# GpSimd's scatter of edge sums waits for 24 of 98 merging steps, in place of the first

## What is computed

```
h = relu(layernorm(x)); x = x + L0(h, edges)          # two rounds of messages, summed per node, then a GRU cell
h = relu(layernorm(x)); x = x + L1(h, edges, weight)  # weighted sum over the edges of a node
h = relu(layernorm(x)); x = x + L2(h, src, dst)       # attention: softmax over the edges of a node
h = relu(layernorm(x)); x = x + L3(h, edges)          # mean over the edges of a node, two dense products
...
agg[n] = sum of msg[e] over the edges e with dst[e] == n
```

## Time and profile before

| | |
|---|---|
| time, three runs | 3922.49, 3908.88, 3908.34 us; median 3908.88 |
| span of the profiled execution | 3922.1 us |
| the run nearest to that span | 3922.49 us, 0.4 above it |
| GpSimd's scatter, first to last start | 71.0 to 1168.1 us |
| merging steps, first to last `summed` | 70.6 to 1113.9 us |
| table loads begin (L428) | 1187.05 us |

### The profile page before, as it was taken

One profiled execution on the slowest core, in us unless ns is written; L12 is line 12 of the kernel. 1 busy time (PEld: TensorE's weight loads), 2 busy tenths in 40 slices (PEclk: granted clock), 3 DMA queues, 4 the chain that ended last, 5 costly groups with the idle time before them and its releaser, 6 DMA issues.

```text
span 3922.1 us, 37110 instructions
## 1 busy us (share of the span) xinstructions
PE 2203.3 (56%) x11497; PEld 1368.2 (35%) x11497; DVE 1745.8 (45%) x2706; ACT 981.7 (25%) x1791; POOL 1607.2 (41%) x1664
## 2 busy tenths in 40 slices
PE   3111111111113666678989677777777777777389
PEld 2000000000001132454544455555555555555245
DVE  6121112111126223343423367666666666766742
ACT  0000000000001322200110145555555555555311
POOL 2766666666670000002000455555555555555300
PEclk7555555555555778878999788888888888888689
DMA  9999200000003978763358577777887777777443
GB/s 389 368 333 366 90 1 2 1 1 2 1 6 137 403 297 325 266 190 96 109 188 259 163 209 215 215 218 212 221 225 211 211 218 213 217 213 217 130 134 113
DMA packets 509104, 724.18 MB, mean 185 GB/s; under 512 B 70756, under 2 KB 366621, under 8 KB 509008
## 3 DMA queue, kind: packets, MB, share of 16 engines
q1 hardware_dynamic: 437444, 608.72, 47.2%
q0 software_dynamic: 65680, 109.05, 10.9%
q10 hardware_dynamic: 5884, 5.21, 0.4%
HBM read 402.27 MB, written 320.51 MB: 184 GB/s over the span
## 4 chain that ended last, share of the span: by engine, by line
PE 36%; another core or an unknown queue 28%; DVE 12%; issue 9%; DMA 8%; ACT 7%; SPq 0%; ACTq 0%; POOL 0%; DVEq 0%; POOLq 0%
PE PS L677 8%; DMA G<-adj_d 7%; PE PS L981 5%; PE PS L951 4%; PE PS L960 4%; PE PS L976 3%; PE PS L1006 2%; DVE V L1648 2%; PE PS L811 2%; PE PS L975 1%; DVE V L1649 1%; ACT OSF L1266 1%; ACT M L1259 1%; ACT D L1277 1%
## 5 line engine op out<-in xcount | busy, mean ns | idle before, releaser
L595 POOL DMA_INDIRECT G<-tab_sv,src_e x784 | 768.3, 980 | 648.7 <-PE PS L677 395.5
L605 POOL DMA_INDIRECT adj_d<-D,place x782 | 752.9, 963 | 410.3 <-issue 240.7
L733 PE MATMUL PS<-G,V 128*128 128x4 bf16 x391 | 41.8, 171 | 885.3 <-issue 488.5
L981 PE MATMUL PS<-M,ident 128*128 128x512 f32 x392 | 272.7, 785 | 334.3 <-ACT M L1259 247.4
L733 PEld LDWEIGHTS PS<-G,V 128*128 128x128 bf16 x391 | 33.6, 104 | 973.0 <-issue 529.2
L1656 DVE TENSOR_REDUCE D<-PS 128x8 f32<-128x24 f32 x98 | 17.5, 178 | 714.7 <-remote 710.8
L1955 DVE TENSOR_TENSOR_SCAN RB<-mring,RB,PS 128x512 f32<-128x512 bf16 x196 | 250.3, 1277 | 139.3 <-PE PS L981 132.6
L1935 DVE TENSOR_TENSOR_SCAN HTx<-PS,HTx,D 128x512 f32<-128x512 f32 x196 | 250.9, 1280 | 90.7 <-remote 49.2
L976 PE MATMUL PS<-VT 128*128 128x128 f32 x1568 | 287.1, 285 | 0.0
L595 POOL DMA_INDIRECT wlast<-wsum_d,last_i x25 | 23.9, 957 | 627.7 <-DVE last_i L1867 620.4
L1266 ACT ACTIVATE OSF<-PS 128x512 f32<-128x512 f32 x392 | 212.3, 593 | 269.9 <-PE PS L677 160.6
(11 more groups left out here) (402 smaller groups left out, 4694.3 us busy)
## 6 DMA issues: line engine op xcount, KB each, us to landing
frac_d<-OSF SPq DMA_DIRECT2D x196, 512.0 KB
adj_d<-RB SPq DMA_DIRECT2D x7, 12800.0 KB, 44.0
G<-adj_d SPq DMA_DIRECT2D x161, 512.0 KB, 6.1
run_d<-RB SPq DMA_DIRECT2D x4, 12992.0 KB
VT<-run_d SPq DMA_DIRECT2D x196, 256.0 KB
wts_d<-X SPq DMA_DIRECT2D x149, 256.0 KB, 6.3
mring<-cut_d SPq DMA_DIRECT2D x196, 128.0 KB
HTx<-seg_d SPq DMA_DIRECT2D x196, 128.0 KB
```

The costliest lines, as they stand in the source:

```text
L595: pool.indirect_dma_start(dest, None, table, bass.IndirectOffsetOnAxis(ap=idx, axis=0)).then_inc(done, 16)
L605: pool.indirect_dma_start(adj_d, bass.IndirectOffsetOnAxis(ap=place[:, 2 * w + k:2 * w + k + 1], axis=0), pay[:, w, k, :], None).then_inc( ...
L981: nc.tensor.matmul(PS[:, q, :], ident[:, :], Ee[:, q, :], start=False, stop=True, skip_group_check=True).then_inc(leaky, 1)
```

## The change

GpSimd's wait for `summed` before a window of a new step asks for at least 24. The first DMA of the scatter so waits for 24 merging steps (96 of 391 windows) in place of one, and all waits up to the 24th step are met from then on. From the 24th step on each wait asks for what it asked before. No instruction is added, removed or moved on any engine.

```diff
@@ -62,6 +62,7 @@
 NU = 2 * NSG
 NP = -(-NW // 4)
+AHEAD = 24
 PC = 512
@@ -616,7 +617,7 @@
                     for w in windows(u):
                         if w % 4 == 0 or w == windows(u)[0]:
-                            pool.wait_ge(summed, w // 4 + 1)
+                            pool.wait_ge(summed, max(w // 4 + 1, AHEAD))
                         issue(0, u, w)
```

## The result

| | before | changed |
|---|---|---|
| median of five runs | 3908.88 us | 3954.48 us |
| lowest to highest | 3896.95 to 3922.52 | 3936.16 to 3960.43 |
| span of the profiled run | 3922.1 us | 3934.4 us |
| scatter, first to last start | 71.0 to 1168.1 | 115.5 to 1213.3 |

The change makes the kernel slower: ratio 1.0102, 95% interval 1.0066 to 1.0138, 45.6 us between the medians. The two profiled runs are 12.3 us apart only: that of the changed kernel was the fastest of its five, that of before lay 13.6 above its median. The scatter's end says more than the spans do: it moved by 45.3 us.

A forecast was written before the change was run, and what follows sets the result against it. The prediction took the scatter to be bound by GpSimd's own issuing, with merging a tenth of it. A start 43.5 us later and 41 us of saved pauses gave +2 us, a forecast of 3911 us, range 3885 to 3953.

The forecast's parts named there:

- The likeliest case, no change: Whole kernel: late start and saved pauses nearly cancel, +2 us, time 3911 us; chance of "same" 0.61.
- slow rival: Scatter: the start costs its 43.5 us and nothing comes back, 3952 us; chance 0.21.
- What bounds the kernel: Scatter of edge sums: bound by GpSimd's own issuing, a tenth by merging; its end moves later loads and layers one for one.
- The start: GpSimd's first scatter DMA: waits for 24 merging steps at 1.89 us, begins at 114.5 in place of 71.0, +43.5 us.
- The pauses saved: Scatter up to the 286th DMA: GpSimd doesn't pause until the margin is used up, -41 us.
- The meeting point: Scatter: GpSimd catches up with merging at step 38, the 286th DMA, at 475 us.
- about one instruction for each of its DMAs: Merging beside the unbroken scatter: TensorE completes that many after a reserve of four or five quick steps; 36 us a step taken.
- From the meeting on both kernels stand alike: no margin, a pause every some 50 DMAs, to the end: Scatter after the 286th DMA: nothing differs but the phase, one pause of up to 8 us more or less.
- a mild form of the slow rival: Scatter after the meeting: GpSimd's later pauses grow by more than 18 us; counted within the slow rival's 0.21.
- The slow rival's own mechanism: Merging: the profiler's recording holds TensorE's completions; in timed runs merging stays ahead at 1.89 us a step, without pauses.
- Merging keeps up: Scatter: with the margin GpSimd never pauses, +43.5 - 110 = -67 us, 3842 us; chance 0.17.

The follow-up runs named there:

- few24: The changed kernel with the third small matmul of each window left out, 20 TensorE instructions a merging step in place of 28; 3966.21 us, ratio to before 1.0115.
- a48b: The kernel before with GpSimd's first wait asking for 48 merging steps, on the third chip, which holds TensorE; 4029.41 us, ratio to before 1.0196.
- before2: The kernel before, unchanged, profiled again on the first chip, which doesn't hold TensorE; 2885.29 us, ratio to itself 0.9996.
- few1: The kernel before with the third small matmul of each window left out, 20 TensorE instructions a merging step; 3949.15 us, ratio 1.0000.
- before3: The kernel before, unchanged, executed once for a third profile on the third chip, which holds TensorE; 3945.0 us.

## Why the prediction was right or wrong

The forecast was 3911 with a range of 3885 to 3953, the measured median 3954.5: 1.5 above the range's end by these five runs, within it by the ratio (3908.9 x 1.0102 = 3948.8). The likeliest case, no change, was wrong; the slow side, given 0.21, came. That the range reached so far up is not to the account's credit: it was stretched for a slow rival whose mechanism isn't what the runs showed (5).

1. *What bounds the kernel*: right on a chip that holds TensorE. The scatter's end moved by 45.3 us and the time by about as much (34 to 46 us in two sessions). One for one it holds only within the 20 us by which the chain behind the scatter varies (18, 37 and 17 us in three profiles).
2. *The start*: forecast +43.5, measured +44.5; 1.89 us a step held for 24 steps in a row.
3. *The pauses saved*: forecast 41 us up to the 286th DMA, measured 28.6 up to the 288th. The meeting point was right (286 and 288), but by luck: the steps took 39.2 us where I took 36, which alone puts the meeting at about the 277th DMA, and GpSimd's own slowing put it back. The term was mis-sized because I let GpSimd run at 1.263 us a DMA: 375.4/288 is 1.303, since in a long stretch it too is slowed. few24's 20 DMAs in 28.0 us and a48b's 336 in 470.4 show that slowing by itself. The prediction's "about one instruction for each of its DMAs" is wrong too: the price is 1.40 us an instruction, with 31 DMAs in a step of 28 instructions as with 28.
4. *"From the meeting on both kernels stand alike: no margin, a pause every some 50 DMAs, to the end"*: this is the step that failed. The runs showed a debt there: pauses of 14.6 and 14.7 us in the changed kernel, three in few24, one of 21 and one of 7 in a48b, after which GpSimd was as late as its start had been. In place of "alike", the changed kernel's first 302 DMAs ended with the whole 45.3 us of the late start, and the scatter's length came out as before (1097.8 and 1097.0 us): none of the 41 us of saved pauses was kept. I had named later pauses growing by more than 18 us as a mild form of the slow rival, and hadn't priced it.
5. *The slow rival's own mechanism*, that the pauses are a product of the recording: not borne out. before2 is a profile as the others are, and has no pauses; and on the other chips executions that weren't profiled take as long as the profiled ones (medians of 3919 and 3950 us). On before2's chip the rival's arithmetic is exact (+45.6 for a start 45.3 later).
6. *Merging keeps up*: it does on one chip of three, and there isn't a pause to be saved.

**What stays open.** Why some chips hold TensorE to one instruction in 1.40 us beside GpSimd's DMAs and one doesn't; what the two share; and what sets the 1.40 us for both. few1 shows that the sum of the pauses doesn't go by TensorE's instruction count; the account above, by which they give back what GpSimd has run ahead, fits the numbers and is not shown. The same kernel took 2886 us on one chip and 3920 to 3950 on two others, and this is not explained.

(The Trainium skill, page SBUF — State Buffer, section on its two separate sides, says that only the port pair of VectorE and GpSimd can cause contention among the engines. before2 agrees, with steps of 1.89 us beside the scatter. On the two chips that hold TensorE a step takes 39.2 us. If that hold were at a port of SBUF, page and rows would differ, and the rows would decide; no run here shows where it is.)

## What to carry to other kernels

A head start for a producer doesn't help a consumer that is bound by its own pace: it starts later by the whole of it. That held here with the producer quick and, which I had not expected, with it slow: the time that a consumer spends waiting is not all there to be saved, since the scatter took no longer with 113 us of pauses than with 98 (before and changed, idle gaps over 1 us), and 12 us longer with 123 than with 56 (before3 and a48b). Measure the distance of the two kernels at the same instruction of the bounding engine at several points, since at the 288th DMA this change looked like 16 us and at the 302nd like 45. And profile on more than one chip before you call a wait part of the kernel.

## What the runs showed of the hardware

On two of the three chips tried after the first session, and in the first session, TensorE completed one instruction (a weight load or a matmul) in 1.40 us once GpSimd had issued some 25 to 50 indirect DMAs without a pause: 39.2 us for 28 instructions, 28.0 us for 20. In the same time GpSimd issued 31 DMAs (22 for the 20 instructions) at 1.26 us, and 28 (20) at 1.40 us once some 200 had gone without a pause. VectorE's and ScalarE's waits for TensorE's results got longer by that, VectorE's by up to 31.9 us, though the trace lists the matmuls as issued long before. On the third chip the same program shows no such hold, and takes 2886 us where it takes 3909 to 3950 elsewhere.
